# Four-block Flamingo-style network on one core: the epsilon of four layer norms moves from VectorE to GpSimd, and the feed-forward's scale constants are multiplied together once

## The reference

```python
x = x + tanh(g_xattn[0]) * ssm(ctx, layernorm(x))        # a Mamba scan over the context, gated by silu of the norm
x = x + tanh(g_ffn[0])   * bitnet_ffn(layernorm(x))      # gate and value, ternary weights, int8 rows, hidden 2048
x = x + tanh(g_xattn[1]) * cross_attention(layernorm(x), ctx)   # 16 heads of 128, rmsnorm on q and k
x = x + tanh(g_ffn[1])   * experts(layernorm(x))         # 4 experts by token index, hidden 512

def _layernorm(x, axis=-1, eps=1e-05):
    m = jnp.mean(x, axis=axis, keepdims=True)
    v = jnp.var(x, axis=axis, keepdims=True)
    return (x - m) / jnp.sqrt(v + eps)
```

## Time and profile before

| | |
|---|---|
| median of 3 runs | 1925.34 us (1918.67 to 1925.84) |
| profiled execution | 1920.75 us, of which the span of the trace is 1918.8 us |
| granted TensorE clock, mean | 0.963 |
| busy: PE, DVE, ACT, POOL | 1770.7, 1385.1, 977.4, 629.1 us |
| 128 x 1 instructions of VectorE at L846 | 64, of 153 to 154 ns |
| `power` on 128 x 1 at GpSimd (L1392) | 64, from 538 ns |

### The profile page before, as it was taken

The page is one execution under the profiler, slowest core; times in us unless marked ns, Lnnn a source line. Parts: engine busy times, 40 slices in busy tenths (PEclk is TensorE's granted clock), DMA queues, the critical chain, the costliest instruction groups (busy, mean ns, idle before and its releaser), DMA issues.

```text
span 1918.8 us, 19484 instructions
## 1 busy us (share of the span) xinstructions
PE 1770.7 (92%) x6054; PEld 808.7 (42%) x6054; DVE 1385.1 (72%) x2088; ACT 977.4 (51%) x1922; POOL 629.1 (33%) x613
## 2 busy tenths in 40 slices
PE   7338999997999899999999979999999999999999
PEld 3113343443444344444434434444445334444543
DVE  2897877998998899899988999997753444432221
ACT  6995655565664464666456455664435333330100
POOL 0024431136653224554432245563203332320000
PEclk9659999998999999999999989999999999999999
DMA  7689973279783115797521458971103599865210
GB/s 255 188 210 271 274 221 122 90 213 236 188 201 102 35 44 121 176 259 191 143 73 43 98 130 205 239 182 63 46 23 99 181 282 266 240 171 210 86 50 33
DMA packets 163173, 300.30 MB, mean 157 GB/s; under 512 B 18936, under 2 KB 51704, under 8 KB 160128
## 3 DMA queue, kind: packets, MB, share of 16 engines
q1 hardware_dynamic: 145792, 236.14, 39.7%
q0 software_dynamic: 17280, 62.92, 16.9%
HBM read 177.64 MB, written 58.33 MB: 123 GB/s over the span
## 4 chain that ended last, share of the span: by engine, by line
PE 76%; DVE 10%; ACT 6%; DMA 5%; issue 3%; SPq 1%; POOL 0%; DVEq 0%; ACTq 0%
PE p L775 11%; PE p L765 9%; PE p L745 9%; PE p L728 8%; PE p L707 6%; PE p L812 6%; PE p L621 5%; PE p L702 4%; PE p L751 4%; PE p L827 3%; PE p L668 3%; DVE s_M L943 2%; DMA s_U<-in_Wv 1%; DVE s_U L1083 1%; ACT s_wq L1178 1%
## 5 line engine op out<-in xcount | busy, mean ns | idle before, releaser
L943 DVE TENSOR_TENSOR_SCAN s_M<-s_M 128x1024 f32<-128x1024 f32 x128 | 300.4, 2347 | 15.9 <-ACT s_M L1191 13.1
L1083 DVE CUSTOM_DVE_ANT_0 s_U<-p,s_U 128x512 f32<-128x512 f32 x256 | 187.0, 745 | 148.5 <-PE p L745 144.2
L1408 POOL DMA_DIRECT2D s_u<-s_M x120 | 112.1, 934 | 500.1 <-DVE s_M L948 477.9
L745 PE MATMUL p<-s_U 128*128 128x512 f32 x512 | 267.6, 610 | 8.8 <-DVE s_U L1083 7.1
L728 PE MATMUL p<-s_U 128*128 128x512 f32 x512 | 258.5, 612 | 7.1 <-ACT s_U L1311 3.5
L1453 POOL TENSOR_SCALAR s_U<-s_U 128x512 f32<-128x512 f32 x256 | 232.8, 939 | 5.8
L775 PE MATMUL p<-s_U 128*128 128x512 f32 x512 | 223.6, 593 | 0.0
L765 PE MATMUL p<-s_U 128*128 128x512 f32 x472 | 212.3, 592 | 0.0
L1324 ACT COPY s_U<-p 128x512 f32<-128x512 f32 x196 | 105.6, 592 | 175.5 <-PE p L751 173.6
L1191 ACT ACTIVATE s_M<-s_dl,s_small 128x511 f32<-128x511 f32 x256 | 170.4, 717 | 39.4 <-DVE s_M L943 33.6
L1319 ACT ACTIVATE s_U<-s_U 128x512 f32<-128x512 f32 x256 | 181.6, 710 | 5.4
(11 more groups left out here) (177 smaller groups left out, 2410.4 us busy)
## 6 DMA issues: line engine op xcount, KB each, us to landing
s_u<-s_M POOLq DMA_DIRECT2D x120, 512.0 KB, 7.4
s_bc<-bc_scratch SPq DMA_DIRECT2D x128, 256.0 KB, 4.9
k_scratch<-s_U SPq DMA_DIRECT2D x16, 1024.0 KB, 7.7
v_scratch<-s_U SPq DMA_DIRECT2D x16, 1024.0 KB, 6.7
s_U<-in_Wq SPq DMA_DIRECT2D x64, 256.0 KB, 6.7
s_U<-k_scratch SPq DMA_DIRECT2D x64, 256.0 KB, 5.2
s_U<-in_Wo SPq DMA_DIRECT2D x64, 256.0 KB, 4.2
s_U<-rk_scratch SPq DMA_DIRECT2D x64, 256.0 KB, 5.3
```

Of the source, the lines that this page charges most:

```text
L745: e.matmul(banks[bk][:], qT[j % 3][:, k * 128:(k + 1) * 128], kT[j % 2], start=True, stop=True).then_inc(S["a_s"], 1)
L943: e.tensor_tensor_scan(w, dA[i % 2], w, 0.0, ALU.mult, ALU.add).then_inc(S["m_s"], 1)
L1083: e.tensor_tensor_reduce(out=Pm[j % 2][:, k, :], in0=banks[ABANK[kind, j, k]][:], in1=rkb[j % 2], scale=rq[:, k:k + 1], scalar=-3.0e38, op ...
```

## The change

`rowstat` ends with the aggregation. A new GpSimd helper `deviation` adds the epsilon and then takes the power, with a wait on its own semaphore between the two, in all four norms. Attention's `power` calls stay. The two pairs of semaphores of the feed-forward and the turn become one pair, counted 8 per batch. The feed-forward's constants `0.5/127`, `2/127` and `tanh(g)/127` are multiplied with the three weight scales once into `gsc`, at the first tile. A tile then has two small scale operations after its quantising in place of three, and one after the hidden rows in place of two. `plan()` is untouched, so each engine's order of parts is as it was.

```diff
+        gsc = sb("gsc", [128, 3])
...
             def rowstat(src, dst, tmp, rv):
                 e.bn_stats(tmp, src).then_inc(*v.up())
                 e.wait_ge(*v.now())
-                e.bn_aggr(dst, tmp).then_inc(*v.up())
-                e.wait_ge(*v.now())
-                e.tensor_scalar(dst[:, 1:2], dst[:, 1:2], EPS, None, ALU.add).then_inc(S[rv], 1)
+                e.bn_aggr(dst, tmp).then_inc(S[rv], 1)
...
-                        e.tensor_scalar(qt[:, 12:13], qt[:, 10:11], gam[:, 0:1], 0.5 / 127.0, ALU.mult, ALU.mult).then_inc(*v.up())
-                        e.tensor_scalar(qt[:, 13:14], qt[:, 10:11], gam[:, 1:2], 2.0 / 127.0, ALU.mult, ALU.mult).then_inc(*v.up())
+                        if f == 0:
+                            for k3 in range(2):
+                                e.tensor_scalar(gsc[:, k3:k3 + 1], gam[:, k3:k3 + 1], (0.5, 2.0)[k3] / 127.0, None, ALU.mult).then_inc(*v.up())
+                            e.tensor_scalar(gsc[:, 2:3], gam[:, 2:3], gts[:, 2:3], 1.0 / 127.0, ALU.mult, ALU.mult).then_inc(*v.up())
+                            e.wait_ge(*v.now())
+                        e.tensor_scalar(qt[:, 12:13], qt[:, 10:11], gsc[:, 0:1], None, ALU.mult).then_inc(*v.up())
                         e.wait_ge(*v.now())
-                        e.tensor_tensor(qt[:, 13:14], qt[:, 13:14], qt[:, 12:13], ALU.mult).then_inc(S["f_sc"], 1)
+                        e.scalar_tensor_tensor(qt[:, 13:14], qt[:, 10:11], gsc[:, 1:2], qt[:, 12:13], ALU.mult, ALU.mult).then_inc(S["f_sc"], 1)
...
-                        e.tensor_scalar(qt[:, 20:21], qt[:, 18:19], gam[:, 2:3], 1.0 / 127.0, ALU.mult, ALU.mult).then_inc(*v.up())
-                        e.wait_ge(*v.now())
-                        e.tensor_scalar(qt[:, 20:21], qt[:, 20:21], gts[:, 2:3], None, ALU.mult).then_inc(*v.up())
+                        e.tensor_scalar(qt[:, 20:21], qt[:, 18:19], gsc[:, 2:3], None, ALU.mult).then_inc(*v.up())
...
+            def deviation(ap, wait, done):
+
+                e.wait_ge(*wait)
+                e.tensor_scalar(ap, ap, EPS, 1.0, ALU.add, ALU.mult).then_inc(*v.up())
+                e.wait_ge(*v.now())
+                e.tensor_tensor(ap, ap, mhalf[:, 0:1], ALU.pow).then_inc(S[done], 1)
```

More of the change, by code:

```diff
@@ L29 @@
 f_t f_g f_v f_ht f_o f_x f_th f_hc f_rv f_rs f_hn f_q f_z f_sc f_ob f_pad f_p f_h f_hq f_y
-x_rv x_rs x_hn x_t x_c
+x_hn x_t x_c
 k_k k_v k_n k_kc k_sq k_vc k_nv k_p
@@ L33 @@
 e_xt e_g e_u e_d e_xc e_s e_rv e_rs e_hn e_it e_y
-dve_own act_own
+dve_own act_own pool_own
 d_w0 d_w1 d_w2 d_ipw d_dtw d_const d_small d_c0 d_cr d_x0 d_x1 d_cb d_raw d_rows d_bcw d_bc0 d_bc1
@@ L997, in dve_ffn @@
                             e.wait_ge(S["q_put"], 12)
-                        e.wait_ge(S["f_rs"], f + 1)
+                        e.wait_ge(S["f_rs"], 8 * b + t + 1)
                         e.tensor_scalar(xn, xt, qt[:, 0:1], qt[:, 1:2], ALU.subtract, ALU.mult).then_inc(S["f_hn"], 1)
@@ L1060, in dve_turn @@
                             e.wait_ge(S["f_y"], 4 * b + 4)
-                        rowstat(x[:, t, :], aq[:, 8 * t:8 * t + 2], aq[:, 8 * t + 2:8 * t + 8], "x_rv")
+                        rowstat(x[:, t, :], aq[:, 8 * t:8 * t + 2], aq[:, 8 * t + 2:8 * t + 8], "f_rv")
                     elif kind == "hn":
-                        e.wait_ge(S["x_rs"], 4 * b + t + 1)
+                        e.wait_ge(S["f_rs"], 8 * b + t + 5)
                         e.tensor_scalar(ltmp[t], x[:, t, :], aq[:, 8 * t:8 * t + 1], aq[:, 8 * t + 1:8 * t + 2], ALU.subtract, ALU.mult).then_inc(S["x_hn"], 1)
@@ L1392, in power @@
                 e.tensor_tensor(ap, ap, mhalf[:, 0:ap.shape[1]], ALU.pow).then_inc(S[done], 1)
+            v = Chain(S["pool_own"])
+            def deviation(ap, wait, done):
[3 more added lines that the diff above has]
+                e.tensor_tensor(ap, ap, mhalf[:, 0:1], ALU.pow).then_inc(S[done], 1)
             def pool_quant():
@@ L1400, in pool_mamba @@
                     if kind == "ln":
-                        power(st[:, 8 * i + 1:8 * i + 2], (S["m_rv"], 4 * b + i + 1), "m_rs")
+                        deviation(st[:, 8 * i + 1:8 * i + 2], (S["m_rv"], 4 * b + i + 1), "m_rs")
                     elif kind == "out" and i < 2 * NS - 2:
@@ L1418, in pool_ffn @@
                             e.memset(xb[:, 512:640], 0.0).then_inc(S["f_pad"], 1)
-                        power(qt[:, 1:2], (S["f_rv"], f + 1), "f_rs")
+                        deviation(qt[:, 1:2], (S["f_rv"], 8 * b + t + 1), "f_rs")
                     elif kind == "o":
@@ L1429, in pool_turn @@
                     if kind == "st":
-                        power(aq[:, 8 * t + 1:8 * t + 2], (S["x_rv"], 4 * b + t + 1), "x_rs")
+                        deviation(aq[:, 8 * t + 1:8 * t + 2], (S["f_rv"], 8 * b + t + 5), "f_rs")
                     yield
@@ L1458, in rows @@
                     for b in bs:
-                        power(st[:, 8 * b + 1:8 * b + 2], (S["e_rv"], 4 * ex + b + 1), "e_rs")
+                        deviation(st[:, 8 * b + 1:8 * b + 2], (S["e_rv"], 4 * ex + b + 1), "e_rs")
                 for kind, ex, p in EXP:
```

## The result

The changed kernel takes **1910.23 us** (median of 11 runs, 1905.68 to 1917.97) against 1920.44 us of the kernel before beside it (11 runs, 1910.63 to 1928.23). The ratio is 0.9942, with a 95% interval of 0.9922 to 0.9961: 10 to 11 us or 0.6% faster. Of the 13.3 us between forecast and result, 4.9 have nothing to do with the change: the forecast starts from the median of three runs, 1925.3, and the eleven give 1920.4.

A forecast was written before the change was run, and what follows sets the result against it. TensorE was taken to bound the kernel, with 76% of the chain. Terms -3.8 (VectorE), +1.2 and +0.2 (experts) and +0.6 (tails) gave -1.8 us, so 1925.3 became 1923.5 us; range 1912 to 1935 for 8 in 10.

The forecast's parts named there:

- The step that failed: Mamba's tails, batches 1 to 3: of 12 tiles, one in four pays 0.4 us, 1.2 halved to +0.6 us.
- my own 0.4 us for a deviation: On GpSimd, each deviation grows by 0.3 us of addition plus 0.1 us of semaphore wait (0.2 to 0.8).
- The second rival: Mamba's tails: the power waits out the next scan, delaying attention's scalings and TensorE's transposes; slower, 1935.5 us, chance 0.11.
- The first rival: Whole kernel: VectorE's saved work carries over, 14.8 us less 2.0 us of GpSimd; 1912.5 us, chance 0.15.
- The gain of the epsilon on the chain: VectorE's epsilon addition stands on the chain 16 times; removing it saves 0.21 us each, 3.4 us.
- The successor: On VectorE, the instruction after the aggregation follows it by 0.07 to 0.1 us once the addition is gone.
- The experts' chain of three deviations: First experts' norms, at 1534.44 us: three deviations in a row on the chain cost 3 x 0.4 = 1.2 us.
- VectorE's work: Whole kernel: VectorE about 16 us less busy, its waits on TensorE longer by nearly as much.
- The three-operand form: Feed-forward, replacing the last product: costs 0 to 0.05 us more each, 0.8 us at most, 0.4 taken in all.
- The scale edits: Feed-forward scale operations after the hidden rows: on the chain 3 times at 0.12 us, 0.4 us saved.

The follow-up runs named there:

- e3: Kernel before with the epsilon addition moved to GpSimd in Mamba's tails alone, 16 of 64 additions; ratio 0.9977 (0.9950 to 1.0003).
- c7: Second trace of e3, the kernel before with the epsilon moved in Mamba's tails alone; 1904.37 us.
- e10: Changed kernel keeping only the tails' epsilon move and all scale edits, other epsilon additions on VectorE; ratio 0.9903 (0.9880 to 0.9927) against before.
- c6: Same kernel as e10, traced and timed again; ratio 0.9951 (0.9930 to 0.9972) against before.
- e5: Kernel before, VectorE's epsilon additions kept, with GpSimd adding 0.0 ahead of the power in Mamba's tails; ratio 0.9973 (0.9951 to 0.9996).
- e4: Kernel before with the epsilon of the four norms added on neither engine, power unchanged; ratio 0.9983 (0.9959 to 1.0006).
- e6: Kernel before with the epsilon moved to GpSimd in the feed-forward and at the turn alone, 32 of 64 additions; ratio 0.9994 (0.9970 to 1.0019).
- e2: Scale edits alone: the changed kernel with rowstat and power as before, epsilon on VectorE; ratio 0.9968 (0.9942 to 0.9994) against before.
- c8: Same kernel as e2, scale edits alone, timed again; ratio 0.9978 (0.9960 to 0.9996) against before.
- e9: Changed kernel with the epsilon left on VectorE in Mamba's tails, 48 of 64 additions moved; ratio 0.9964 (0.9943 to 0.9985) against before.
- e12: Changed kernel with the experts' 16 epsilon additions left on VectorE; ratio 0.9945 (0.9924 to 0.9966) against before.
- e1: Epsilon part alone: kernel before with deviation on GpSimd in all four norms, scales unchanged; ratio 0.9953 (0.9929 to 0.9977).

## Why the prediction was wrong

**The step that failed** is the one on Mamba's tails: "Of 12 such tiles I put one in four on the path with the plain 0.4 us, and none with more", a term of +0.6 us. It has the wrong sign. In the changed kernel the tails of batches 1 and 2 give -6.65 and -2.89 us against the first trace of before; the stretch with that of batch 3 costs 0.75 (1240 to 1310 us; 0.74 to 0.78 in all three traces of the change, e3, c7, e10 and c6, 1.45 in e5). So the term is -8.8 us against that trace, and about -7 against the mean of the seven traces without an addition. I had read 4.90 against 2.29 us and the wait behind it, named the port, and asked only how an addition could suffer from it. I never asked who is stretched now and what that costs. GpSimd started 0.31 us ahead of the scan and 0.09 ahead of the product: my own 0.4 us for a deviation was longer than both leads, and with them 2.6 + 2.6 us of VectorE's time and 5.58 us of TensorE's waits were at stake. That belonged among the rivals. The measured shift was larger still, 0.72 and 0.74 us.

**The second rival** had the place and the mechanism with the opposite result: the scalings do start later, which it counted as damage, and TensorE does wait for them now (4.6 us), but that replaces larger waits and a lower clock.

**The first rival** gives 1912.5 us, the time nearest to the result, and is not its cause: e4 makes VectorE's 13.4 us saving without GpSimd's instruction and gets 0.9983 (3.3 us, and its interval holds a gain of nothing). Its test, TensorE's waits on L1083, L985 and L1064 falling by over 8 us, failed too: 18.4 + 6.0 + 5.5 before, 14.2 + 5.2 + 5.6 after, 4.9 less. A time that fits doesn't show a cause.

**What was right.** The gain of the epsilon on the chain was taken at 3.4 us; e4 gives 3.3, but with an interval from 0 to 8 us it is no proof. The successor follows the aggregation by 0.10 us (556.92, 557.02), where I had 0.07 to 0.1. The experts' chain of three deviations was forecast at 3 us in place of 1.77:

```profile
1526.33 0.20 POOL s_st L1400
1526.53 0.07 issue
1526.60 0.56 POOL s_st L1402
...
1528.52 0.64 POOL s_st L1402
1529.15 0.03 issue
1529.18 0.03 DVE s_M L1113
```

From 1526.33 to 1529.15 it is 2.82 us, 1.05 more than before, where I had 1.2. An addition alone takes 0.20 us and its gap 0.07, together 0.27 in place of my 0.4; the estimate of 0.31 us for the addition was too high. VectorE's work fell by 19.9 us, forecast about 16; the products and scans on 128 x 1024, with GpSimd stretching fewer of them, take 6.6 us less, which is more than the rest. TensorE's busy time, forecast unchanged, fell by 5.4 us. VectorE's waits behind the deviations of the feed-forward and turn cost nothing that e6 shows. The three-operand form took 220 ns, 0.01 above my bound.

**What was mis-sized.** The scale edits were worth 0.4 us in my sum. e2 and c8 give 0.32% and 0.22%, 4 to 6 us, and both intervals leave out 1, by little. In their traces I find 0.4 us at 700 to 780 us and nothing else that repeats, so where this gain lies, and how sure its size is, stays open.

**How the parts add up.** By time: tails 0.2 to 0.3% (e3, e5, and the whole against e9), scales 0.2 to 0.3%, together 0.4 to 0.6% of the whole's 0.6. The rest of the epsilon gives nothing in e6 and e12, while e1, with all of the epsilon, has 0.47% against e3's 0.23%; their intervals overlap. By the traces the tails alone give about 7 us or 0.36% (against the mean of the traces without an addition, and less what batch 3 costs), somewhat more than the timings leave of them. Two places where it is given back in some traces are known, 460 to 500 us with 2.6 to 3.1 and, in e3 and e5, 600 to 700 us with +4.95; c7, the same kernel as e3, has neither. How often they happen wasn't measured.

## What to carry to other kernels

Where two engines share a port and one is stretched in the trace (here 4.90 for 2.29 us), look at which of the two is stretched, by how much it started late, and which can afford it: a lead of 0.1 to 0.3 us was turned here by a single small instruction, and the sign of the edit followed from who had slack, not from the work added. Look also at the meetings that cost little (23 of 25 scans here), since starting second doesn't by itself make an instruction long. Then test the two halves of a moved operation apart (removed here, added there); the time of the whole fits several stories. And for effects of half a per cent on a kernel whose runs scatter by one, compare stretches by the index of the same matrix product, take a second trace of the kernel before as well (one stretch of it differed by 2.6 us), and time the candidate twice before it is called better.

## What the runs showed of the hardware

- A GpSimd instruction ahead of a meeting made two stretches 6.18 and 2.42 us shorter with no work removed: 16 additions of 0.0 in e5, 0.9973 (0.9951 to 0.9996) by time.
- In Mamba's tail of batch 1 the scan takes 4.90 or 4.76 us behind the start of four scalings and 2.29 ahead of them; the four scalings take 5.33 us behind the scan and 2.69 ahead of it (e4). Elsewhere a scan that starts behind a scaling takes at most 2.66 us in 23 of 25 cases (before).
- GpSimd's addition on 128 x 1 takes 0.18 to 0.20 us alone, near VectorE's 0.154, and up to 1.75 us (567.41, changed kernel) beside VectorE's work.
- After the same wait of 2.2 us at about 650 us, TensorE's granted clock at 660 to 680 us was 0.74 in one trace of a kernel and 1.00 in another (e3, c7); at 640 to 660 us it was 0.91 in both.
